# A hybrid layer on one core: the first feed-forward's first head woven into attention's last steps, and the units of both feed-forward halves as one stream with four banks

## The reference, cut

```python
x = x + attention(layernorm(x))
x = x + ffn(layernorm(x))            # "f1"
x = x + mamba(layernorm(x))
x = x + ffn(layernorm(x))            # "f2", the same weights as f1
...
# attention: 16 heads of 8 columns, 1024 rows each, for 2 batches
logits = einsum('bhld,bhmd->bhlm', q, k) * scale + bias[None]
out    = einsum('bhlm,bhmd->bhld', softmax(logits), v)
...
# ffn: 64 experts of width 64, the best 8 of the best 4 groups of 8, and a shared one of width 256
scores = sigmoid(xf @ router_w.T);  sfc = scores + correction_bias
...                                  # top 2 per group, top 4 groups, top 8 experts: tw, tidx
tw = tw / (tw.sum(-1) + 1e-20) * 2.5
routed = sum over experts e of combine[:, e] * (relu(xf @ up_w[e])**2 @ down_w[e])
return routed + relu(xf @ shared_up_w)**2 @ shared_down_w
```

## Time and profile before

| | us |
|---|---|
| median of 3 runs | 1153.76 |
| lowest, highest | 1152.01, 1156.81 |
| the profiled execution | 1157.08 |
| span of its trace | 1155.3 |
| attention | 0 to 493.6 |
| f1: head, units, tail | 495.0 to 526.65, to 741.7, to 751.6 |
| mamba | 753 to 897.6 |
| f2: head, units, drain | 899.3 to 930.8, to 1144.1, to 1155.3 |

### The profile page before, as it was taken

How to read it: one execution, slowest core, us unless ns; L and a number is a source line. 1 busy time by engine, 2 the same in 40 slices (tenths; PEclk the granted TensorE clock), 3 DMA queues, 4 the chain that set the end, 5 groups by cost and what they waited for, 6 DMA issues and landing times. The chain is left out here.

```text
span 1155.3 us, 16936 instructions
## 1 busy us (share of the span) xinstructions
PE 984.0 (85%) x5500; PEld 532.8 (46%) x5500; DVE 823.1 (71%) x2168; ACT 687.9 (60%) x1057; POOL 493.3 (43%) x456
## 2 busy tenths in 40 slices
PE   3789999999999999826989999873777278899998
PEld 1222222222222222215668678631566256686886
DVE  6778999999999997066874454477897668644453
ACT  5236656666656656624667788667334146687886
POOL 3400100110111100003778799814774047787997
PEclk9769999999999999957999999987899579899999
DMA  4910322133023300005455576300000055465763
GB/s 100 321 51 15 101 70 51 47 112 80 21 74 88 83 1 2 1 3 122 144 144 175 130 190 189 93 20 0 0 0 1 3 135 142 137 184 132 204 193 96
DMA packets 79862, 105.58 MB, mean 91 GB/s; under 512 B 17581, under 2 KB 40867, under 8 KB 79779
## 3 DMA queue, kind: packets, MB, share of 16 engines
q1 hardware_dynamic: 77420, 101.96, 32.8%
q10 hardware_dynamic: 2358, 2.60, 0.8%
HBM read 95.77 MB, written 8.52 MB: 90 GB/s over the span
## 5 line engine op out<-in xcount | busy, mean ns | idle before, releaser
L475 POOL TENSOR_TENSOR f_act_low<-f_act,f_act_high 128x512 fp32r<-128x512 f32 x272 | 352.9, 1305 | 128.5 <-ACT f_act_high L439 112.7
L1380 DVE CUSTOM_DVE_ANT_0 at_rows<-at_rows,at_table_max 128x512 f32<-128x512 f32 x512 | 339.8, 719 | 41.2 <-PE at_rows L1176 40.1
L1332 ACT ACTIVATE at_prob<-at_cols 128x1024 f32<-128x1024 f32 x256 | 248.1, 1021 | 162.5 <-PE at_cols L1210 162.5
L591 DVE SCALAR_TENSOR_TENSOR f_gated<-f_hid,f_cw 128x512 f32<-128x512 f32 x256 | 176.4, 690 | 155.2 <-PE f_hid L379 151.8
L446 ACT ACTIVATE f_act<-f_gated 128x512 f32<-128x512 f32 x272 | 172.0, 632 | 112.7 <-DVE f_gated L591 91.1
L439 ACT CAST f_act_high<-f_act 128x512 fp32r<-128x512 f32 x272 | 164.1, 605 | 0.0
L1222 PE MATMUL at_pv<-at_prob,at_v_stack 128*32 128x512 f32 x1024 | 137.2, 608 | 0.6 <-ACT at_prob L1332 0.6
L1210 PE MATMUL at_cols<-at_table_cols,flip_sum 128*64 128x512 f16 x1024 | 137.2, 389 | 0.0
L1176 PE MATMUL at_rows<-at_k_stack,at_q_stack 48*128 48x512 bf16 x512 | 119.1, 398 | 18.2 <-DVE at_maxima L1380 12.5
L379 PE MATMUL f_hid<-f_x_high,wu_high 128*128 128x512 f32 x272 | 115.9, 426 | 15.3 <-DVE f_gated L591 12.7
L386 PE MATMUL f_acc<-f_act_high,wd_high 128*128 128x512 f32 x272 | 112.9, 415 | 8.1 <-POOL f_act_low L475 7.9
(11 more groups left out here) (261 smaller groups left out, 1180.9 us busy)
## 6 DMA issues: line engine op xcount, KB each, us to landing
f_cw<-f_c_rows SPq DMA_DIRECT2D x256, 256.0 KB, 4.4
at_table_cols<-bias_rows SPq DMA_DIRECT2D x32, 248.0 KB, 5.3
at_table_max<-bias_rows SPq DMA_DIRECT2D x12, 480.0 KB, 4.5
at_q_stack<-q_parts SPq DMA_DIRECT2D x28, 96.0 KB, 2.4
at_k_stack<-k_parts SPq DMA_DIRECT2D x24, 96.0 KB, 3.5
at_raw_weights<-in_L_ffn_up_w_dram SPq DMA_DIRECT2D x8, 256.0 KB, 4.3
at_raw_weights<-in_L_ffn_down_w_dram SPq DMA_DIRECT2D x8, 256.0 KB, 4.8
at_table_max<-bias_rows ACTq DMA_DIRECT2D x4, 480.0 KB, 6.6
```

What stands on the lines that cost most here:

```text
L475: nc.gpsimd.tensor_tensor(act_l[:, n % PART_SLOTS, :], act[:, n % ACT_SLOTS, :], act_h[:, n % PART_SLOTS, :].bitcast(F32), ALU.subtract).t ...
L591: ins = nc.vector.scalar_tensor_tensor(out=gated[:, n % 3, :], in0=hid[:, n % 2, :], scalar=0.0, in1=cw[:, (k + b * PAIRS) % C_SLOTS, n % ...
L1332: act(prob[:, S % 2, 2 * hp:2 * hp + 2, :], s2[:, hp, :, :], ACT.Exp).then_inc(exp_done, 1)
L1380: nc.vector.tensor_tensor_reduce(out=slot, in0=slot, in1=t_max[:, 2 * p.hp + j, c:c + BANK][:, ::-1], scale=1.0, scalar=-3.0e38, op0=ALU.a ...
```

## The change

1. **Attention's start.** The high parts of the first two kinds of q and k are made by VectorE rather than ScalarE; the stack loads of q go to SyncE's queue, the loads of the maxima tables are issued by ScalarE together; the second batch's four projections all come before the first pair; an Exp on one column (`warm`) comes before the steps.
2. **Turned outputs.** `turn_outputs` multiplies by a 0/1 matrix `pick` of 36 columns, and so writes only the 36 columns that are used, in place of transposes of 128.
3. **Steps without pairs** go score, bias, score, bias.
4. **Head of f1's first half** runs in attention's last steps on all engines, in attention's own tiles (`v_nat`, the raw weights) and the two free slots of `s1`; its score is an Exp with VectorE's 1/(1+e) in place of the sigmoid; the root and what follows stand after the last step. Its shares are stored by SyncE at attention's end, and f1 begins with units.
5. **One stream.** The 136 units of both halves are one loop: LAG 5, four `hid` banks, two `acc` banks that the halves share; the down of half 1's first pair waits for the copy of half 0's outputs. Head 1 is woven by a new table, its reciprocal cut in four, and both parts of x and the router's copy are VectorE's.

```diff
+        for t in range(QT):
+            last = mm(s1[:, bank, t * OUT_COLS:(t + 1) * OUT_COLS], oT[:, t * P:(t + 1) * P],
+                      m.pick[:].rearrange("p h e -> p (h e)"), start=True, stop=True)
-                    last = nc.tensor.transpose(s1[:, at % SLOTS, t * P:(t + 1) * P], oT[:, t * P:(t + 1) * P],
-                                               m.ident[:])
...
+AMONG_UNITS = HeadPlan(var=1, rows=(3, 5), turn=(5, 7), logits=(10, 11, 12, 13), score=14, route=16, every=1.4,
+                       root=46, newton=48)
+AMONG_STEPS = HeadPlan(var=115, rows=(116, 116), turn=(117, 117), logits=(118, 118, 118, 118), score=118, route=119,
+                       every=0.38, root=129, newton=129)
...
+        if self.spare:
+            nc.scalar.activation(score, self.logit_bank, ACT.Exp, scale=-1.0).then_inc(self.score_ready, 1)
+        else:
+            nc.scalar.activation(score, self.logit_bank, ACT.Sigmoid).then_inc(self.score_ready, 1)
...
+            if not self.spare:
+                yield at.turn[j] + 1
+                v.wait_ge(self.xnT_ready, j + 1)
+                nc.vector.tensor_copy(self.xh[:, cols], t.xnT[:, cols]).then_inc(self.x_high, 1)
+                v.wait_ge(self.x_high, j + 1)
+                tt(self.xl[:, cols], t.xnT[:, cols], self.xh[:, cols].bitcast(F32), ALU.subtract).then_inc(self.x_low, 1)
...
+        for k in range(0, HT, 2):
+            ch.add(nc.vector.reciprocal(sfc[:, k:k + 2, :], sfc[:, k:k + 2, :]))
+            place += 1
+            yield place
...
+            def up(unit):
+                n, cols = unit.n, slice(unit.j * BANK, (unit.j + 1) * BANK)
+                if n % FFN_UNITS == 0 and heads[unit.b]:
+                    pe.wait_ge(heads[unit.b].x_low, QH)
+                if n >= HID_SLOTS:
+                    pe.wait_ge(u.gate_done, n - HID_SLOTS + 1)
...
+                pe.wait_ge(u.low_done, n + 1)
+                if unit.b and unit.pp == 0:
+                    pe.wait_ge(u.outT_ready, unit.j + 1)
...
-            weave(units(eng, 0), head(eng, 1))
-            weave(units(eng, 1), tail(eng, 0))
-            run(tail(eng, 1))
+            if heads[0]:
+                run(head(heads[0], eng))
+            weave(units(eng), side())
...
+                    else:
+                        for hp in range(2):
+                            scores(S, hp)
+                            biases(S, hp)
...
+            @block.scalar
+            def _(a):
+                weave(scalar_program(a), head.scalar_program(a))
...
+        moe_ffn(m, "f1", router_w, correction_bias, rows[0], first_done=True)
```

More of the change, by code:

```diff
@@ new lines, in moe_ffn, with __init__ @@
+        four = sb("routing", [P, 4, HT, E_ALL])
+        tiles = HeadTiles(sb, sb("xn", [P, HT, D])[:], sb("xnT", [D, TH])[:], [four[:, k, :, :] for k in range(4)])
+        banks = ((misc[:, 0, :], misc[:, 1, :]), misc[:, 0, :], misc[:, 1, :])
+        heads = [None if first_done and b == 0 else
+                 FfnHead(m, tag, b, tiles, router, xh[b][:], xl[b][:], c_rows, banks, AMONG_UNITS) for b in range(HALVES)]
+        heads[1].before = heads[0]
+        u = FfnUnits(m, tag)
+        class Unit:
+            def __init__(self, n):
+                self.n, self.b, i = n, n // FFN_UNITS, n % FFN_UNITS
+                self.pp, self.j = i // QH, i % QH
+                self.q = QH * self.b + self.j
+                self.share = self.b * PAIRS + self.pp - SHARED if self.pp >= SHARED else None
@@ L736, in __init__ @@
         self.take(("out", PHASES - 1), 1)
+        self.pairs_over = self.start["maxima", PHASES - 1]
+        self.out_bank = self.pairs_over % SLOTS
+        self.others = [k for k in range(SLOTS) if k != self.out_bank]
     def take(self, key, slots):
@@ L833, in attention @@
         allot_weights(m)
+        m.x0 = [m.sb(f"x0_{k}", [D, TH], F32R, early) for k in ("high", "low")]
         m.stage = stage
@@ L884, in attention @@
         slots = Slots()
+        router = Router(m, sb, "at")
+        tiles = HeadTiles(sb, v_nat[:, 0:HT, :], v_nat[:, HT:NT, :].rearrange("p t d -> p (t d)"),
+                          [raw[:, i, j, :].rearrange("p (t e) -> p t e", e=E_ALL) for i in range(2) for j in range(2)])
+        free = [s1[:, k, :] for k in slots.others]
+        entry = {"var": (stats_taken, LT), "rows": (v_ready, ITERS), "turn": (slots_free, slots.pairs_over),
+                 "score": (raw_low, 2 * len(WEIGHT_STEPS))}
+        head = FfnHead(m, "f1", 0, tiles, router, m.x0[0][:], m.x0[1][:], c_rows, (free, free[1], free[0]),
+                       AMONG_STEPS, entry, spare=True)
         KINDS = 2 * NQ
@@ L989, in _ @@
                 load_k(sp, 0, 0, 0, L)
+                for lh in range(2):
+                    load_q(sp, 0, 0, lh)
+                router.load(sp, router_w, correction_bias)
                 sp.wait_ge(b_lo_ready, 1)
@@ L1228, in _ @@
                 more = second_batch()
+                next(more)
                 for n in range(AHEAD):
```

772 lines of the change are left out of this document (409 added, 363 removed).

## The result

The changed kernel takes 1119.8 us (median of 4; 1118.0 to 1122.1) against 1154.9 for before (median of 4): a ratio of 0.970, 95% interval 0.967 to 0.973. So it gained 35 us, where 56 were forecast, and lies just outside the range of 1085 to 1118. The direction was right; the size wasn't. Where the missing 21 us are is the question of what follows.

A forecast was written before the change was run, and what follows sets the result against it. PE bounds the kernel except in the heads and the streams' waits. Terms -4.5 + 5 - 18.8 - 20.6 - 17.0 = -55.9 took 1157.1 to 1101.2, and 3.3 for the profiled run gave 1098; range 1085 to 1118.

The forecast's parts named there:

- Attention's start, -4.5: Attention up to the first step: maxima done earlier (-3.6), Exp's table load gone (-1.3), 0.4 lost on q's loads.
- After that nothing stands between pairs, and VectorE's own pace is the bound: Attention's start, after the first pair: VectorE's 44 maxima at 0.65 set the pace, ending at 66.0 rather than 69.6.
- The upper bound of +1: Attention's start: the worst case, if the q stack on SP comes later by the projections' gain.
- Turns, +5: Turned outputs in attention's steps: eight instructions for four delay fourteen phases, up to 0.36 added each; range 0 to +8.
- The head and the last steps, -18.8: Attention's last steps to f1's first unit: reached at 507.8 rather than 526.65; bounds -24 and -8.
- The stalls of 6.4: Last steps: the woven head costs +4.0 for table loads and PE's turns, +2.4 for logits and the router's copy.
- the serial rest: After attention's last row: root, reciprocal to share (5.7 with the root), turn 1.0, copy 0.7, store 2.0, block end 1.5.
- The gain per step: Steps without pairs: score and bias in turn start the first Exp earlier, 11 x 0.38, -4.2.
- The streams, -39.5: Unit streams of both feed-forwards: -20.6 in f1 (215.0 to 194.4), -18.9 in f2 (213.3 to 194.4).
- the first rival: Streams: VectorE and GpSimd in each other's way, two-input operations 1.31 rather than 0.42; total 1110 to 1118; chance 0.15.
- small stalls, 3: Streams: part of the lost time that stays, beside 2.6 for the low clock and 3.7 for turns and logits.
- The four banks bring nothing: Streams: if GpSimd's chain from gate to low part binds, they keep 207 and 205; total 1123; chance 0.04.

The follow-up runs named there:

- e16b: Changed kernel with f2's parts of x in one tile of 2048 columns for both halves rather than a tile for each half; 1114.2 us, a single run.
- e4: Changed kernel with two hid banks in place of four, all else as it is; 1118.6 us (1117.1 to 1125.1).

## Why the prediction was wrong, point by point

- **What bounds the kernel**: right. The two streams' lost time and the head were where the gain was to be had.
- **Attention's start, -4.5**: the eight profiles that keep the clock come nearer to it (-1.8 to -4.1 at the first products, e16b's the last), the change's own doesn't (+2.4 there, +1.1 at step 4). The middle of the 14 is -1.8. The failed step is "After that nothing stands between pairs, and VectorE's own pace is the bound": the v products stand between them, and at the low clock they make PE the bound. The upper bound of +1 was too low. A sum is off as well: 8.3 of projections less 5.2 of wait are 3.1, not 1.3. The projections took 6.3, since the clock rose at 34.6, and so the first pair came 2.4 later, of which 1.45 is the wait for the stack.
- **Turns, +5**: right in kind and near in size: 0.43 a phase where 0.36 was taken, 5.1 between steps 4 and 112 and 6.4 in all. The rest of the +6.6 is the collision at step 76, which the prediction didn't know of.
- **The head and the last steps, -18.8**: 16.4 measured, or 17.3 without the two turned phases that fall into the stretch. The stalls of 6.4 were sized rightly (6.3), and the serial rest came out to a microsecond (21.9 for 21.0). The gain per step wasn't: 0.23 for 0.38. The head by itself did better than its terms, 16.2 for 14.6.
- **The streams, -39.5**: 28.0. This is the large miss, and its cause is the first rival. The mis-sized term is "small stalls, 3": from unit 8 to 56 alone the streams lost 9.8 and 8.4. The row of 0.42 and 1.31 stood in the prediction; what I didn't do is count the operations that it applies to and put them into the forecast. In f2 21 operations waited for GpSimd's subtraction, 15 us together; they make VectorE the bound for 40 us, and banks don't help against that. The rival's own wording was off in one thing: GpSimd was not at its limit (32.9 of 40), VectorE was.
- **Luck in the streams**: the miss of 11.5 is flattered. At the changed kernel's own pace 265 half-units of 0.680 are 180.2, so 20 us stay lost in each stream where the forecast left 9.3. The faster pace, which nobody forecast and no run explained, gave back 5 in each. Without it the miss would be 21, a little above the 12 to 20 that the first rival asked.
- **"The four banks bring nothing"**, given 0.04, is what e4 shows, though not for its reason, GpSimd's chain (and its terms add up to 1121, not 1123). That the streams still fell by 14 came from the faster pace (5.0), the one stream without border, the wait at the reciprocal with its low clock that is gone, and a little from the lag.
- **The range**: its upper end of 1118 took the first rival alone. The start and the attention steps came on top of it.

## What to carry to other kernels

Before pricing an operation that moves under other work, look up what it takes when the other engine is busy, and count all operations of its kind that can meet it; an operation of 24 columns can cost nearly as much as one of 256. Where VectorE and GpSimd worked side by side here, one operand in PSUM was worth more than more buffers: 7 to 8 us for two banks that brought nothing as buffers. Two more banks covered 0.9 us of one long operation; they didn't help against an engine that was behind for forty microseconds.

Compare a change by the stretch that it touches. A stream's first units and attention's start move by 3 and 6 us from one execution to the next, more than most of these edits.

## What the runs showed that I had not expected

- Undisturbed units take 1.360 in all variants of the changed kernel and 1.397 in all of before, 5 us in each stream, and no run shows why.
- The same instructions at attention's start end 6.5 us apart from one profile to the next, by whether the clock falls to 1.2 GHz at 38 us or holds to 51. A single profile of a change there says little.
- PE takes 0.13 us for each float32 instruction of 36, 64 or 128 columns in the rows above (0.15 for the four transposes of a phase), so that fewer columns in more instructions lost here.
